# The third layer on per-node sums of second-layer units, for one of the two ways, with that way's bias and relu on VectorE

## What is computed

```python
def _mlp(x, w1, b1, w2, b2, w3, b3):        # 384 -> 256 -> 256 -> 128
    x = relu(x @ w1.T + b1)
    x = relu(x @ w2.T + b2)
    return x @ w3.T + b3
def _prop_once(node_states, f_idx, t_idx, edge_features, ...):
    edge_inputs = concatenate([node_states[f_idx], node_states[t_idx], edge_features], axis=1)
    edge_states = _mlp(edge_inputs, w1, b1, w2, b2, w3, b3)
    return segment_sum(edge_states, t_idx, num_segments=3125)
agg = _prop_once(x, src, dst, ...) + _prop_once(x, dst, src, ...)
```

## Time and profile before

| | |
|---|---|
| time, median of 3 runs | 2317.35 us (2312.87 to 2318.26) |
| the profiled execution | 2316.54 us, of which span 2314.8 us |
| granted TensorE clock, mean | 0.994 of full |
| PE busy | 2257.0 us |
| DVE busy | 1762.0 us |
| ACT busy | 1231.7 us |
| POOL busy | 1182.7 us |
| chain that ended last | PE 92%, DMA 3%, DVE 2% |

### The profile page before, as it was taken

One profiled execution on the slowest core, in us unless ns is written; L12 is line 12 of the kernel. 1 busy time (PEld: TensorE's weight loads), 2 busy tenths in 40 slices (PEclk: granted clock), 3 DMA queues, 4 the chain that ended last, 5 costly groups with the idle time before them and its releaser, 6 DMA issues.

```text
span 2314.8 us, 38789 instructions
## 1 busy us (share of the span) xinstructions
PE 2257.0 (98%) x12559; PEld 1831.4 (79%) x12559; DVE 1762.0 (76%) x4035; ACT 1231.7 (53%) x2118; POOL 1182.7 (51%) x858
## 2 busy tenths in 40 slices
PE   4999999999999999999999999999999999899997
PEld 3888888888888888888888888888888874587775
DVE  7888888888888888888888888888888856703112
ACT  4565666566666656665666566656656543411122
POOL 2566666666566656665666666666656640001100
PEclk9999999999999999999999999999999999999999
DMA  4356454455445554554554445444545339286965
GB/s 163 71 113 125 98 106 92 88 112 101 91 89 106 99 98 91 108 97 89 100 112 93 88 98 107 99 89 104 101 89 99 72 62 268 94 351 258 384 263 189
DMA packets 242547, 292.52 MB, mean 126 GB/s; under 512 B 126757, under 2 KB 200056, under 8 KB 234385
## 3 DMA queue, kind: packets, MB, share of 16 engines
q1 hardware_dynamic: 168194, 236.50, 33.9%
q0 software_dynamic: 73216, 54.58, 18.0%
q10 hardware_dynamic: 1040, 0.52, 0.1%
HBM read 218.43 MB, written 73.08 MB: 126 GB/s over the span
## 4 chain that ended last, share of the span: by engine, by line
PE 92%; DMA 3%; DVE 2%; issue 1%; ACT 1%; POOL 0%; DVEq 0%; SPq 0%; POOLq 0%; ACTq 0%
PE bank L1238 24%; PE bank L1224 18%; PE bank L1250 16%; PE bank L2136 8%; PE bank L1303 4%; PE bank L1282 4%; PE bank L1298 4%; PE bank L1185 4%; DMA l_ring<-adj 2%; PE bank L1801 2%; PE bank L1267 2%; PE bank L1809 1%; PE bank L1268 1%; PE bank L2150 1%; PE bank L2159 1%
## 5 line engine op out<-in xcount | busy, mean ns | idle before, releaser
L495 POOL DMA_INDIRECT sums<-outb,target x416 | 667.3, 1604 | 590.8 <-ACT outb L666 456.8
L488 POOL DMA_INDIRECT xg<-in_x,gidx x416 | 489.3, 1176 | 148.3 <-issue 137.1
L1250 PEld LDWEIGHTS bank<-w3t,h 128*128 128x128 f32 x3328 | 387.5, 192 | 8.8 <-issue 0.2
L1250 PE MATMUL bank<-w3t,h 128*128 128x128 f32 x3328 | 388.3, 275 | 0.1
L1238 PE MATMUL bank<-h1h,w2h 128*128 128x512 f32 x832 | 365.5, 439 | 3.3 <-DVE h1l L861 3.3
L648 ACT ACTIVATE h<-bank,b2c 128x512 f32<-128x512 f32 x416 | 286.2, 688 | 122.2 <-PE bank L1238 122.2
L634 ACT ACTIVATE h1h<-hpre 128x512 fp32r<-128x512 f32 x416 | 257.8, 628 | 171.9 <-DVE hpre L857 171.9
L1238 PE MATMUL bank<-h1h,w2l 128*128 128x512 f32 x832 | 328.8, 395 | 0.0
L1238 PE MATMUL bank<-h1l,w2h 128*128 128x512 f32 x832 | 328.5, 395 | 0.0
L861 DVE SCALAR_TENSOR_TENSOR h1l<-hpre,h1h 128x512 fp32r<-128x512 f32 x416 | 268.6, 687 | 16.8 <-ACT h1h L634 16.8
L857 DVE TENSOR_TENSOR hpre<-pb,bank 128x512 f32<-128x512 f32 x416 | 264.9, 676 | 2.3 <-PE bank L1224 2.1
(11 more groups left out here) (263 smaller groups left out, 3695.6 us busy)
## 6 DMA issues: line engine op xcount, KB each, us to landing
l_ring<-adj SPq DMA_DIRECT2D x54, 1568.0 KB, 8.2
rowb<-along SPq DMA_DIRECT2D x104, 512.0 KB, 4.4
ef<-in_edge_attr SPq DMA_DIRECT2D x103, 256.0 KB, 2.7
adj<-band SPq DMA_DIRECT2D x46, 480.0 KB
adj<-band SPq DMA_DIRECT2D x23, 540.0 KB
stay<-adj SPq DMA_DIRECT2D x6, 1568.0 KB, 14.8
xg<-in_x,gidx POOLq DMA_INDIRECT x416
sums<-outb,target POOLq DMA_INDIRECT x416, 4.0
```

The costliest lines, as they stand in the source:

```text
L488: pool.indirect_dma_start(out=to, out_offset=None, in_=a["x"], in_offset=bass.IndirectOffsetOnAxis(ap=ids, axis=0)).then_inc(s_x[par], 16)
L495: pool.indirect_dma_start(out=tables[k % 2], out_offset=bass.IndirectOffsetOnAxis(ap=target[par][:, 1, k:k + 1], axis=0), in_=outb[par][:, ...
L1250: last = nc.tensor.matmul(bank[6 + way][:, t * P:(t + 1) * P], h2[:, way, k, t * P:(t + 1) * P], w3t[:, k, :], start=not bias and k == 0, ...
```

## The change

In way 0, layer 3 moves behind the sum over edges. The parts:

- Layer 2 of way 0 is computed upright, with edges in partitions: h1 is the stationary operand and w2 the moving one. `upright(g, n)` does two blocks of 128 edges, each by six matmuls of 256 columns.
- With units along the columns the bias isn't one value per partition. DVE (not ACT) computes max(z, -b2), which is relu(z + b2) - b2, into `he` (the half of h2 that way 0 had). What is subtracted is given back at the end through b3 and the degrees: w3 b2 is added to b3.
- `third` runs for way 1 alone. `total` sums both halves of way 0's units (8 matmuls of 64 columns, not 4), and `deliver` adds them to aggw and to a second array aggv. Layer 3 is applied to these at the end, in `last_layer`; DVE then copies instead of adding.
- For space, h1l lies over hpre (one `Slab`), aggv over tiles that only `general()` uses, es is halved. The weights are loaded by 9 DMAs instead of 6, ACT clears aggv, and four DVE steps of the preamble move to `general()`.

The diff, cut to the windowed branch; what is left out are the same changes of names and waits for `general()`, and the tiles' places:

```diff
                 def results(g):
...
+                    if win:
+                        act.wait_ge(s_l3, g + 1)
+                        act.wait_ge(s_sum, g * 2)
+                        nc.scalar.copy(es[:, :], bank[7][:, :]).then_inc(s_es, 1)
...
                 def turn(g, par, turns, ahead=2, early=False, cleared=None):
                     if win and ahead:
                         xs_out(g + 1)
-                    second(g, 0)
+                    if not win:
+                        second(g, 0)
                     if ahead:
                         upper_sd(g + 1)
-                    second(g, 1)
+                    if not win:
+                        second(g, 1)
...
                 def both(f):
                     dve.wait_ge(s_pc, g * HB + (f + 1))
                     dve.wait_ge(s_q, g * HB + (f + 1))
+                    if f == 0:
+                        dve.wait_ge(s_l2, g * 4)
...
+                def upright(g, n):
+
+                    if isinstance(g, int) and g == 0:
+                        dve.wait_ge(s_b2, 1)
+                    else:
+                        dve.wait_ge(s_sum, g * 2 - 1)
+                    dve.wait_ge(s_l2, g * 4 + (n + 1))
+                    nc.vector.tensor_tensor(he[:, 2 * n:2 * n + 2, :], bank[6 + n][:, :].rearrange("p (t u) -> p t u", t=2),
+                                            b2row[:, :].unsqueeze(1).broadcast_to([P, 2, H]), ALU.max).then_inc(s_he, 1)
+
                 def deliver(g):
...
                     part = aggw[:, bass.ds(g * PACE, SPAN)]
-                    nc.vector.tensor_tensor(part, part, bank[0][:, 0:SPAN], ALU.add).then_inc(s_agg, 1)
+                    nc.vector.tensor_tensor(part, part, bank[0][:, 0:SPAN], ALU.add)
+                    part = aggv[:, bass.ds(g * PACE, SPAN)]
+                    nc.vector.tensor_tensor(part, part, bank[0][:, SPAN:2 * SPAN], ALU.add).then_inc(s_agg, 1)
 
                 def turn(g, par, turns, ahead=2, early=0, fresh=None, wrapped=None):
                     begin = isinstance(g, int) and g == 0
                     if ahead:
                         nodes(g + 1, 1 - par, early=early == 2)
                         compare(g + 1, 1 - par, turns + par)
+                    upright(g, 0)
                     places(g, par, early=early > 0)
                     if ahead:
                         sums(g + 1)
...
                     count_pairs(g, 0)
                     count_pairs(g, 1)
+                    if not begin:
+                        upright(g, 1)
                     if ahead and not begin:
                         lower_parts(g + 1)
...
+            PARTS2 = [(w, k, h) for k in range(HB) for w, h in ((w2h, "h"), (w2h, "l"), (w2l, "h"))]
...
+                def upright(g, n):
+
+                    if n == 0:
+                        pe.wait_ge(s_h1l, g * 4 + 4)
+                    if not (isinstance(g, int) and g == 0):
+                        if n == 0:
+                            pe.wait_ge(s_h2, g * 2 - 1)
+                        else:
+                            pe.wait_ge(s_es, g)
+                    for t in range(2 * n, 2 * n + 2):
+                        for q, (w, k, h) in enumerate(PARTS2):
+                            last = nc.tensor.matmul(bank[6 + n][:, t % 2 * H:(t % 2 + 1) * H],
+                                                    units_of(h, 0, k, t * P, (t + 1) * P),
+                                                    w[:, k, :, :].rearrange("p f m -> p (f m)"),
+                                                    start=(q == 0), stop=(q == len(PARTS2) - 1))
+                    last.then_inc(s_l2, 1)
+
...
                 def total(g, par):
                     pe.wait_ge(s_cmp, g + 1)
-                    pe.wait_ge(s_es, g * 2 + 1)
-                    for t in range(K):
-                        last = nc.tensor.matmul(bank[0][:, 0:SPAN], es[:, 0, t * P:(t + 1) * P], into[par][:, t, :],
-                                                start=(t == 0), stop=(t == K - 1))
+                    for k in range(HB):
+                        for t in range(K):
+                            last = nc.tensor.matmul(bank[0][:, k * SPAN:(k + 1) * SPAN], he[:, t, k * P:(k + 1) * P],
+                                                    into[par][:, t, :], start=(t == 0), stop=(t == K - 1))
                     last.then_inc(s_sum, 1)
...
                 def turn(g, par, turns, ahead=2, extra=0):
                     begin = isinstance(g, int) and g == 0
-                    second(g, 0)
+                    upright(g, 0)
                     if ahead:
                         turn_sd(g + 1, 1 - par, turns)
...
-                    second(g, 1)
+                    upright(g, 1)
                     if ahead:
                         turn_e(g + 1, 1 - par, turns, extra)
-                    second(g, 2)
-                    second(g, 3)
+                    for n in range(2, 4):
+                        pe.wait_ge(s_he, g * 2 + (n - 1))
+                        second(g, n)
...
-                    third(g)
+                    pe.wait_ge(s_h2, g * 2 + 2)
+                    third(1)
                     total(g, par)
...
-                def last_bias():
+                def last_layer():
 
                     pe.wait_ge(s_degrow, 4 * 16)
                     pe.wait_ge(s_deg, 2)
-                    pe.wait_ge(s_es, G * 2)
+                    pe.wait_ge(s_es, G)
+                    pe.wait_ge(s_agg, G)
                     for n, bk in enumerate((3, 4, 5, 6, 7, 2, 0)):
-                        if bk == 0:
-                            pe.wait_ge(s_agg, G)
                         row = (degree_lo if n < 4 else degree_hi)[0:2, n % 4 * CB:n % 4 * CB + width(n)]
-                        nc.tensor.matmul(bank[bk][:, 0:width(n)], b3r[0:2, :], row, start=True, stop=True).then_inc(s_degp, 1)
+                        nc.tensor.matmul(bank[bk][:, 0:width(n)], b3r[0:2, :], row, start=True, stop=False)
+                        for k, part in enumerate((aggt, aggv[:, BACK:BACK + AW])):
+                            last = nc.tensor.matmul(bank[bk][:, 0:width(n)], w3t[:, k, :], chunk(part, n),
+                                                    start=False, stop=(k == HB - 1))
+                        last.then_inc(s_degp, 1)
```

More of the change, by code:

```diff
@@ L145, in edge_stage @@
         h1h = sb("h1h", [P, 2, HB, GE], f32r)
-        h1l = sb("h1l", [P, 2, HB, GE], f32r)
         h2 = sb("h2", [P, 2, HB, GE])
-        es = sb("es", [P, 2, GE])
+        es = sb("es", [P, GE])
+        sums_at = Slab(nc, ctx, "sums_at", -(-WIDTH_A * 4 // 32) * 32)
+        sums_at.begin()
+        aggv = sums_at.take("aggv", [WIDTH_A])
+        sums_at.begin()
+        g_es = sums_at.take("g_es", [GE])
+        b3p = sums_at.take("b3p", [2, D])
+        b3hl = sums_at.take("b3hl", [K, D], f32r)
+        pairs = [sums_at.take(f"pairs{i}", [K]) for i in range(2)]
+        rowto = [sums_at.take(f"rowto{i}", [2, K], i32) for i in range(2)]
         match = sb("match", [P, K, P])
@@ L158, in edge_stage @@
         sdh = sb("sdh", [P, 3, GE], f32r)
-        hpre = sb("hpre", [P, HB, 2, GE])
+        units = Slab(nc, ctx, "units", HB * 2 * GE * 4)
+        units.begin()
+        hpre = units.take("hpre", [HB, 2, GE])
+        units.begin()
+        h1l = units.take("h1l", [HB, 2, GE], f32r)
         b3r = sb("b3r", [P, D])
@@ L174, in edge_stage @@
         rowb, xg, ef, same, colhot = taken
+        count_i = rowb[0][:, :, :].bitcast(i32).rearrange("p s e -> p (s e)")
+        diag = match[0:G, :, :].rearrange("g k j -> g (k j)")[:, 0:2 * G + 1]
         rows_i = pb[0:G, :, :].bitcast(i32)
@@ L243, in edge_stage @@
         s_l3 = sem("s_l3")
+        s_he = sem("s_he")
+        s_b2 = sem("s_b2")
         s_es = sem("s_es")
@@ L861, in rest @@
                     nc.vector.scalar_tensor_tensor(
-                        out=h1l[:, way, f, :], in0=hpre[:, f, way, :], scalar=0.0,
+                        out=h1l[:, f, way, :], in0=hpre[:, f, way, :], scalar=0.0,
                         in1=h1h[:, way, f, :].bitcast(fp32), op0=ALU.max, op1=ALU.subtract).then_inc(s_h1l, 1)
@@ L1194, in _ @@
             pe.wait_ge(s_diag, 1)
-            nc.tensor.matmul(bank[7][:, 0:2 * G + 1], ones[0:G, :], diag[:, :], start=True, stop=True).then_inc(s_bases, 1)
-            pe.wait_ge(s_wload, 6 * 16)
+            nc.tensor.matmul(bank[7][:, 0:2 * G + 1], ones[0:G, :], diag, start=True, stop=True).then_inc(s_bases, 1)
+            pe.wait_ge(s_wload, 9 * 16)
             pe.wait_ge(s_whalf, 1)
@@ L1226, in first, with units_of @@
                         last.then_inc(signal, 1)
+            PARTS2 = [(w, k, h) for k in range(HB) for w, h in ((w2h, "h"), (w2h, "l"), (w2l, "h"))]
+            def units_of(h, way, k, lo, hi):
+                return h1h[:, way, k, lo:hi] if h == "h" else h1l[:, k, way, lo:hi]
             def second(g, n):
                 way, f = divmod(n, HB)
-                if n == 0:
```

(46 more changed lines are left out.)

107 lines of the change are left out of this document (61 added, 46 removed).

## The result

The changed kernel takes 2403.97 us (median, 2403.21 to 2407.53) against 2315.11 for the kernel before (median of four): a ratio of 1.0388, with a 95% interval of 1.0366 to 1.0409. The profiled execution took 2403.21, of which the span is 2401.5 us, 86.7 more than the 2314.8 of before.

A forecast was written before the change was run, and what follows sets the result against it. PE was taken to bound the kernel, with DVE having some 1.3 us of slack a turn. From the profiled 2316.54, +82.4 for the turns, +9.5 for the end and +1 for the start gave 2409.4 us, range 2370 to 2455.

The forecast's parts named there:

- time 0: Start of the first matmul of second(g,0) on PE, from which the prediction counts one turn, in us.
- The chain of one turn: In the loop, DVE's first maximum waits for PE, then PE's second(g,3) for DVE's second: turn 18.36, +0.72 on 17.64.
- The handover: At second(g,3), semaphore and weight load between DVE's second maximum and PE's first matmul: estimated 0.15 us (0.04 to 0.3).
- The narrow matmul: In upright on PE, a 256-column matmul was taken as 0.12 us, upper bound 0.157.
- Rival (c): Upright's narrow matmuls cost more: at 0.157 each, upright(g,0) is 0.44 longer, 2455 us; chance within a joint 0.10.
- PE alone: PE's own work per turn: -1.79 for third, +0.89 for total, +0.08 for upright, together -0.82 us.
- The second loop: DVE's h1l for the next tile, done at 16.30, is pushed by 1.72 to 18.02; next turn starts about 18.1.
- Irregular stops: DVE's occasional longer waits in the loop, free before, become paid: +0.06 a turn plus 0.02 for others.
- The end: Behind the loop, last_layer does three times last_bias's work: 16.7 us at full clock, exposed, taken as +9.5.
- The start: Before the loop, more DMA issues, aggv cleared in ScalarE's idle time, fewer DVE steps: +1 us, bounds -1 and +3.
- Rival (a): PE stays the bound and the maxima hide, if DVE's upright(g,1) ends before 6.83: 2243 us; chance 0.08.

The follow-up runs named there:

- The last sorted kernel: Against the kernel with DVE's first maximum behind places and second between the count_pairs, last_layer does fourteen 128-row matmuls, then seven 2-row ones: 2270.16 us.
- the kernel of PE's matmuls alone: Against the changed kernel, ScalarE does way 0's relu in place of DVE's maxima, and way 0's layer-2 bias is left out: 2224.22 us.
- the best places tried: Against the changed kernel, DVE's first maximum moved behind places and its second between the two count_pairs: 2268.66 us.
- the ScalarE kernel: Against the changed kernel, ScalarE does way 0's relu in place of DVE's maxima, and a 512-column matmul per bank adds the bias: 2288.18 us.
- the grouped end: Against the kernel with DVE's first maximum behind places and second between the count_pairs, last_layer does its seven 2-row matmuls first: 2270.89 us.

## Why the prediction was right, and where its terms were off

The forecast was 2409.4; the median is 2403.97, 5.4 below it and inside the range. By its steps, counted from time 0:

- **The chain of one turn** held to 0.05 everywhere. First maximum at 1.72, seen 1.76; `match` 2.33, seen 2.37; second maximum 7.53, seen 7.58; `second(g,3)` 8.37, seen 8.32; from there to the next time 0 9.99, seen 10.03; turn 18.36, seen 18.35. DVE's stop of about 0.5 was 0.46, PE's of 1.4 was 1.42. (The prediction says that the first maximum could have begun at 0.94; by its own rows that is the distance from `into` to `match`, the time is 1.22, and the stop of 0.5 is counted from there.)
- **The handover** from DVE to PE at `second(g,3)`, 0.15 in the sum, came from no row. The changed kernel shows 0.06, from the maximum's end at 1022.90 to 1022.96 (the weight load starts at 1022.95). The first matmul behind the stop then takes 0.33 to the next (1023.29) in place of 0.23, which the working had nowhere. That the two nearly cancel is luck.
- **The narrow matmul** was put at 0.12. From 1014.96 to 1016.02 there are nine steps, 1.06 in all, 0.118 each. Rival (c) was wrong on this term. Each of these matmuls has a load of its own over all 128 rows, which starts while the matmul before it runs: the one for the matmul at 1014.96 starts at 1014.84, with that before it (timeline, PEld). In spite of twice as many loads a matmul takes but 0.118.
- **PE alone** was put at -0.82; the kernel without maxima and bias shows -1.0. Of the missing 0.2, 0.07 is `upright`: a group was put 0.04 longer than six matmuls of 512 columns, and the first one takes 1.49 (1014.64 to 1016.13) where those took 1.48 (1008.21 to 1009.69). Another 0.06 is way 1's sums, 0.86 (1032.13 to 1032.99) in place of 0.92. The last few hundredths I can't place.
- **The second loop**, h1l, was given as 18.02 and came at 17.74 (1032.38 - 1014.64). It didn't bind.
- **A third loop was missing**, sdl and `first`. It changed nothing in the forecast, since in this order the wait at `second(g,3)` hid it; but it made the undoing of that wait nearly worthless (18.2 and 18.1 where I expected 18.05 and 17.65), and with it any advice built on the two loops that I had.
- **Irregular stops** were put at +0.08 a turn, 8.2 us. The 103 turns give 76.1, of which 103 x 0.72 = 74.2 are the regular part: 1.9 remain, and the turns at the two ends explain them: the first is 2.2 longer (17.82 before, 20.02 after) and the last, which the prediction counted as ordinary, 2.1 (12.97 and 15.08). The 101 between them give 71.8, 0.71 each. In these the waits of 1.09 ahead of the second L988, which I had made paid, are nearly gone (L1011 waits 37.5 in 50 times, 0.75 each). What there is instead I had not thought of: four turns of 20.2 to 20.3, in which the clock fell (in one of them to 0.57 over 4 us, below), some 4 x 1.9 = 7.6 us, made up in part by 8 turns of 17.8 to 17.9, and in part because the kernel before had irregular turns of its own (13 of 17.9 and 8 of 18.1).
- **The end** was put at +9.5 and is +12.6: `last_layer` takes 18.64 in place of 16.7, +11.2 on the 7.40 of `last_bias`; the 16 matmuls of the last `total`, counted in no turn, +0.9; a DMA wait +0.5. The 1.9 in `last_layer` is the price of changing between 2-row and 128-row matmuls: I had three times 0.886 a chunk, and a chunk took 2.97. The last sorted kernel gives 0.86 for a 128-row one and (1846.91 - 1843.28)/4 = 0.91 for a 2-row one among their like, 2.63 together. The 9.5 is 9.3 (16.7 less the 7.4 of `last_bias`) and 0.2 for a lost clock. No run shows the 0.2: the changed kernel's `last_layer` had a granted clock of 1.00 from 1968.41 to 1987.05, and the one that did lose it took 23.59. In `last_bias` PE had no gap (busy all of 1888.87 to 1896.27), and the clock was 1.00 from 1888.87 to 1892.40 and 0.50 from 1892.40 to 1896.27, in the middle of the 2-row matmuls.

A chunk of `last_layer` in the changed kernel (timeline, PE):

```profile
1968.41 1.12 PE L1413 MATMUL bank<-hpre,b3r 2*128 2x512 f32 x2 [0.48 <-DMA sdh<-degrees]
1969.46 1.13 PE L1415 MATMUL bank<-aggw,w3t 128*128 128x512 f32 x2
1970.42 1.02 PE L1415 MATMUL bank<-aggv,w3t 128*128 128x512 f32 x2
1971.37 1.12 PE L1413 MATMUL bank<-hpre,b3r 2*128 2x512 f32 x2
```

- **What followed gave 4.1 back**, which no term had. The transposes of wn are 1.5 shorter, 3.43 long at part clock before (0.57 from 1896.27 to 1899.70) and 1.97 after (1.00 from 1987.05 to 1989.02), but only 0.55 of that is left at the first matmul of the last stage that uses `l_ring` (2025.88 and 2116.11). The other 3.55 come in that last stage, where PE waited for the DMAs of `l_ring` 4.0 us in 8 times before and 1.1 in 3 after. What made these land earlier against PE stays open.
- **The start** was put at +1 and is +2.0. Its parts were not taken apart.

Against the profiled 2403.21 the sum was 6.2 too high: 6.3 too much for the irregular stops and 4.1 for what follows the end, less 3.1 and 1.0 too little for end and start. That the sum is nearer than its terms is luck.

Rival (a), that PE stays the bound, had the right size (2243 in its sum; 2224 for the kernel of PE's matmuls alone) and the wrong condition: its test, "ends before 6.83", named one of two consumers, and sdl is the other. Even the best places tried leave a wait for sdl (2268.66); only with the maxima away from DVE was PE the bound.

## To carry to other kernels

When work goes from a full engine to one at 86%, it isn't the share that decides but the queue: for each operation added, follow everything behind it to every consumer on the other engine, and then remove the worst wait on paper and look for the next one, since two waits of nearly the same lateness hide each other. An added operation belongs behind the work that can go on without it, and best into a stop that the engine has for reasons of its own; here two moved lines turned +3.9% into -2.0%.

## What the runs showed of the hardware that I had not expected

**The clock can fall behind a stop in the middle of the loop.** In some turns of the changed kernel PE stood still longer than the usual 1.42, seven times for 1.76 to 1.78. Behind one such stop (timeline, then the stretches around it):

```profile
1003.03 0.50 PE L1280 MATMUL bank<-h1h,w2h 128*128 128x512 f32 x1 [1.78 <-DVE h L1030]
```

```profile
1000.00:1003.00 3.00, 1.25 (x6) 0.69 (x4) 1.95 (x5) 2.00 (x3) 2.39 (x3) 1.00 0.71 235
1003.00:1007.00 4.00, 3.97 (x10) 3.15 (x11) 4.00 (x13) 1.36 (x3) 3.39 (x3) 0.57 1.24 227
1007.00:1010.00 3.00, 3.00 (x14) 2.44 (x13) 1.81 (x6) 1.88 (x4) 1.40 (x2) 1.00 0.63 61
```

the granted clock is 0.57 over these 4 us, most of them at 0.50 (1003.50 to 1006.80), and matmuls of 512 columns come 0.43 apart, not 0.23; the turn takes 20.2. Behind the stop of 1.42 twenty microseconds later the matmuls come 0.23 apart, at a clock of 1.00 (1022.96 to 1026.00). It isn't the length of the stop alone that decides: four of the seven stops of 1.76 to 1.78 have such a fall behind them (turns of 20.2 to 20.3), and three, at 540.28, 1298.30 and 1427.03, have none (turns of 18.7). What tells them apart no run shows. So a wait of PE can cost twice, its length and what the clock takes afterwards. The end of the ScalarE kernel shows the same behind a wait for a DMA (its L1418 is the 2-row matmul; then the stretch):

```profile
1834.48 1.51 PE L1418 MATMUL bank<-hpre,b3r 2*128 2x512 f32 x2 [1.14 <-DMA sdh<-degrees]
```

```profile
1835.00:1845.00 10.00, 10.00 (x12) 2.85 (x10) 0.69 (x1) 0.00 (x0) 6.05 (x4) 0.50 0.31 27
```

**Changing the number of rows costs time.** The chunk of one 2-row and two 128-row matmuls took 2.97 where the same three among their like take 2.63: 0.34 for its two changes. The first number is the changed kernel's, the second comes from the experiments on the end; both are of fp32 matmuls only. The load behind such a change starts with its matmul and not 0.43 ahead of it (1969.45 for 1969.46, against 1969.99 for 1970.42). And **in a run of 2-row matmuls the clock falls** although PE is busy throughout: it did so in all three kernels that have one, in `last_bias` before (0.50 from 1892.40), in the grouped end (0.50 from 1838.20) and behind the 128-row ones (0.70 from 1844.50 to 1850.00).
